# Hyena adapter kernel: loads moved across the two seams between its stages, stores awaited later

## The reference, cut to what matters

```python
def reference(x, ...):
    n = layernorm(x)
    proj = (n @ in_proj_w + in_proj_b).reshape(B, L, C, 3)
    v = depthwise_conv3(proj[..., 0], short_w) + short_b       # along the sequence
    coefs = MLP(pos)                                           # three layers, GELU; (L, C, 2)
    conv = irfft(rfft(v, 2L) * rfft(coefs[..., 1], 2L))[:L]    # the last of two orders decides
    x = x + (proj[..., 2] * conv) @ out_w + out_b
    Wsel, bsel = W[ids], b[ids]                                # 8 of 32 adapters
    return x + einsum('k,kod,bsd->bso', weights, Wsel, layernorm(x)) + weights @ bsel
```

## Time and profile before

| | |
|---|---|
| median of 3 runs | 2428.93 us (2424.77 to 2429.24) |
| profiled execution, its own time | 2427.41 us |
| its span | 2425.2 us |
| first stage and preparation | to 1013.7 us |
| middle, first to last matmul of its groups | 1027.1 to 1442.0 us |
| last stage, from its first matmul | 1455.0 us |
| granted TensorE clock, mean | 0.979 |

### The profile page before, as it was taken

One profiled execution on the slowest core, in us unless ns is written; L12 is line 12 of the kernel. 1 busy time (PEld: TensorE's weight loads), 2 busy tenths in 40 slices (PEclk: granted clock), 3 DMA queues, 4 the chain that ended last, 5 costly groups with the idle time before them and its releaser, 6 DMA issues. The chain is left out here.

```text
span 2425.2 us, 39710 instructions
## 1 busy us (share of the span) xinstructions
PE 2317.4 (96%) x12804; PEld 1602.1 (66%) x12804; DVE 1553.6 (64%) x2188; ACT 843.5 (35%) x1151; POOL 942.7 (39%) x1189
## 2 busy tenths in 40 slices
PE   6779999999999999779999988999999999999998
PEld 2257777777777777534444435777777777777776
DVE  5834444343434444257777767888888888888886
ACT  3334444444444444334444441222222222222222
POOL 1322222222222222100000006777777777777774
PEclk9879999999999999889999998999999999999999
DMA  5534545445444546489999988766666556665653
GB/s 184 217 100 139 186 165 178 160 154 196 156 160 145 190 153 212 158 337 356 361 355 358 359 315 257 227 182 177 179 177 181 174 175 179 175 176 177 179 179 103
DMA packets 180517, 496.60 MB, mean 205 GB/s; under 512 B 19419, under 2 KB 19740, under 8 KB 159332
## 3 DMA queue, kind: packets, MB, share of 16 engines
q1 hardware_dynamic: 150756, 395.10, 50.7%
q10 hardware_dynamic: 29696, 100.68, 11.5%
HBM read 276.27 MB, written 219.43 MB: 204 GB/s over the span
## 5 line engine op out<-in xcount | busy, mean ns | idle before, releaser
L1055 DVE TENSOR_TENSOR m_m<-m_psA,m_spec 128x1024 f32<-128x1024 f32 x256 | 295.4, 1216 | 132.0 <-PE m_psA L960 128.6
L709 POOL TENSOR_TENSOR vl<-v,vh 128x512 fp32r<-128x512 f32 x128 | 165.2, 1291 | 390.0 <-ACT vh L663 390.0
L1222 ACT ACTIVATE b_zh<-b_psT 128x512 fp32r<-128x512 f32 x128 | 76.5, 597 | 636.8 <-PE b_psT L1271 636.8
L977 PE MATMUL m_psW<-m_m,mats 64*64 64x512 f32 x2048 | 249.6, 593 | 0.0
L960 PE MATMUL m_psA<-m_xin,mats 64*64 64x512 f32 x1536 | 203.9, 602 | 30.5 <-DMA m_xin<-spec_f 13.5
L181 PE MATMUL psV<-wvh,nth 128*128 128x512 f32 x512 | 213.6, 417 | 0.6 <-DVE ntl L791 0.6
L810 DVE TENSOR_TENSOR gto<-psG,bgr 128x512 f32<-128x512 f32 x128 | 87.7, 685 | 195.5 <-PE psG L183 195.4
L181 PE MATMUL b_psO<-woh,b_oh 128*128 128x512 f32 x512 | 211.2, 412 | 0.0
L181 PE MATMUL b_psF<-wfh,b_zh 128*128 128x512 f32 x512 | 207.6, 406 | 2.8 <-DVE b_zl L1324 2.8
L1191 POOL TENSOR_TENSOR b_corr<-b_edge,b_v 128x512 f32<-128x512 f32 x128 | 199.2, 1556 | 14.5 <-DMA b_edge<-edge_f 14.4
L182 PE MATMUL b_psF<-wfl,b_zh 128*128 128x512 f32 x512 | 201.3, 393 | 0.0
(11 more groups left out here) (122 smaller groups left out, 4494.6 us busy)
## 6 DMA issues: line engine op xcount, KB each, us to landing
spec<-fs1o SPq DMA_DIRECT2D x64, 1024.0 KB, 8.8
spec<-m_wo ACTq DMA_DIRECT2D x64, 1024.0 KB, 8.4
b_fin<-spec SPq DMA_DIRECT2D x128, 512.0 KB, 4.6
m_xin<-spec SPq DMA_DIRECT2D x31, 2048.0 KB, 11.8
xg<-in_L_attn_x_dram SPq DMA_DIRECT2D x64, 512.0 KB, 6.1
gate_d<-gto SPq DMA_DIRECT2D x32, 1024.0 KB, 3.9
b_gin<-gate_d SPq DMA_DIRECT2D x128, 256.0 KB, 3.6
b_xin<-in_L_attn_x_dram SPq DMA_DIRECT2D x256, 128.0 KB, 3.2
```

Source lines behind the costliest of these rows:

```text
L709: pool.tensor_tensor(vl[:, t % 2], v[:, t % 2], vh[:, t % 2].bitcast(F32), ALU.subtract).then_inc(v_lo, 1)
L977: mm = pe.matmul(psW[pair % 2][half[slot], q, :], ws[slot][half[q]], m[half[q], pair % RM, part, slot, :], start=part == 0, stop=part == 1)
L1055: dve.tensor_tensor(m[:, (k - 2) % RM, part], psA[k % RA][:], spec[:, par, part], ALU.mult).then_inc(m_done, 1)
```

## The change

- xin, mats and the store tile of the middle ("wide") are allocated once, on the right side of SBUF, for front and middle; front's fs1o and the middle's m_wo are the same memory.
- load_first_groups, in front's list with lag 11, at tiles 2 and 5 of the last sequence: it loads mats and, for groups 0 and 1, spec_f and the seven batches that are stored by then. Batch 7 of both is loaded at the start of the middle, after a wait on the spec1 stores.
- front's SP no longer waits for the spec1 and gate stores at its end.
- The four pieces of group 0's load and load_consts are gone. out_w is loaded at step 0 of the last pass, behind group 30's load (load_w), and split during group 31: the high part by ACT (w_high), the low part by POOL.
- Behind group 31's load SP issues s4, the first row of v0, the edge rows of two tiles (EARLY), the two bias rows, the identity, and gate and x of two tiles; then, after waits, ad_mix and b_fin of two tiles. Their tiles are held from the middle to the last stage. The middle's own waits at its end are gone.
- ad_mix is turned in the last stage, in steps 1 and 3 of the first sequence (turn_w, w_high, w_low), in psF and in the memory of b_res. The other seven rows of v0 are loaded at tiles 9 to 15 of the first sequence.

```diff
--- before.py
+++ after.py
     def front(fc, mc):
...
-            s1o = sb("fs1o", [P, 2, 2, SUB, C])
+            s1o = mc["wide"].rearrange("p s (h t) c -> p s h t c", h=2)
...
+                def load_first_groups(b, t):
+
+                    if not (isinstance(b, int) and b == B - 1 and t in (2, 5)):
+                        return
+                    g = (2, 5).index(t)
+                    if g == 0:
+                        for slot in range(2):
+                            sp.wait_ge(s_stored[slot], 32 * (B - 1) * Q // 2)
+                        sp.dma_start(mc["mats"][:], consts["mid"]).then_inc(mc["mats_in"], 16)
+                    rows = slice(g * P, (g + 1) * P)
+                    sp.dma_start(mc["xin"][:, g, B], spec_f[rows]).then_inc(mc["early_in"][g], 16)
+                    sp.dma_start(mc["xin"][:, g, 0:B - 1], spec1[rows, 0:B - 1]).then_inc(mc["early_in"][g], 16)
...
-                pipelined(sp, B, T, [(load_x, 0), (save_v0, 5), (load_adapter, 6), (store_gate, 8), (store, 9), (store_mix, 11)])
+                pipelined(sp, B, T, [(load_x, 0), (save_v0, 5), (load_adapter, 6), (store_gate, 8), (store, 9), (store_mix, 11), (load_first_groups, 11)])
                 sp.wait_ge(ad_stored, 32)
-                for slot in range(2):
-                    sp.wait_ge(s_stored[slot], 32 * B * Q // 2)
-                    sp.wait_ge(g_stored[slot], 16 * B * Q // 2)
                 sp.wait_ge(v0_out, 16 * B)
...
     def middle(bc, mc):
...
             @block.sync
             def _(sp):
-                sp.dma_start(mats[:], consts["mid"]).then_inc(small_in, 16)
+                for slot in range(2):
+                    sp.wait_ge(mc["s_stored"][slot], 32 * B * Q // 2)
+                for g in range(2):
+                    sp.dma_start(xin[:, g, B - 1], rows_of(spec1, g)[:, B - 1]).then_inc(last_in[g], 16)
+                for slot in range(2):
+                    sp.wait_ge(mc["g_stored"][slot], 16 * B * Q // 2)
...
+                def load_w(i, s):
+
+                    if isinstance(i, int) and i > 0 and s == 0:
+                        sp.dma_start(wraw[:], out_w.rearrange("(k p) c -> p k c", p=P)).then_inc(w_in, 16)
+
+                pipelined(sp, GROUPS // 2, S, [(load, 0), (load_w, 0)])
+
+                sp.dma_start(bc["s4"][:], consts["s4"]).then_inc(bc["s4_in"], 16)
+                sp.dma_start(bc["v0_first"][:], first_v[0].rearrange("(a c) -> a c", a=1).partition_broadcast(P)).then_inc(bc["v0_in"], 16)
+                for t in range(EARLY):
+                    for q in range(2):
+                        sp.dma_start(bc["edge_a"][:, t, q], edge_f[q][:, t * C:(t + 1) * C]).then_inc(bc["edge_in"][t], 16)
+                sp.dma_start(bc["bor"][:], out_b.rearrange("(a c) -> a c", a=1).partition_broadcast(P)).then_inc(bc["rows_in"], 16)
+                sp.dma_start(bc["bfr"][:], ad_bias).then_inc(bc["rows_in"], 16)
+                sp.dma_start(bc["ident"][:], consts["ident"]).then_inc(bc["ident_in"], 16)
+                for t in range(EARLY):
+                    sp.dma_start(bc["gin"][:, t], gate_d[0, t // SUB].rearrange("p (s c) -> s p c", s=SUB)[t % SUB]).then_inc(bc["g_in"][t], 16)
+                    for h in range(2):
+                        sp.dma_start(bc["xin"][h * N1:(h + 1) * N1, t], by_tile(x[0])[h, :, t]).then_inc(bc["x_in"][t], 16)
+                sp.wait_ge(low, 1)
+                sp.dma_start(wraw[:], ad_mix).then_inc(bc["ad_in"], 16)
+                for par in range(2):
+                    sp.wait_ge(stored[0][par], 16 * GROUPS // 2)
+                for t in range(EARLY):
+                    sp.dma_start(bc["fin"][:, t], spec3.rearrange("(r h t) b c -> b t r h c", h=2, t=T)[0, t]).then_inc(bc["f_in"][t], 16)
+
+            @block.gpsimd
+            def _(pool):
+                pool.wait_ge(high, 1)
+                pool.tensor_tensor(bc["wol"][:], wraw[:], bc["woh"][:].bitcast(F32), ALU.subtract).then_inc(low, 1)
...
+                        if k == GS - 1 and at_first(i, s, 2):
+                            pe.wait_ge(last_in[par], 16)
...
-                pe.wait_ge(consts_in, 16 * CONSTS)
-                pe.wait_ge(m_done, 2 * GROUPS * PAIRS)
-                for d in range(CT):
-                    for ot in range(CT):
-                        mm = pe.transpose(psA[d // 2][:, d % 2, ot * P:(ot + 1) * P], ad_raw[:, ot, d * P:(d + 1) * P], bc["ident"][:])
-                    mm.then_inc(turned, 1)
...
+                def w_high(i, s):
+
+                    if isinstance(i, int) and i > 0 and s == GS:
+                        act.wait_ge(w_in, 16)
+                        act.activation(bc["woh"][:], wraw[:], ACT.Copy).then_inc(high, 1)
+
+                pipelined(act, GROUPS // 2, S, [(spectrum, 0), (out_early, 2), (out_last, 3), (w_high, 3)])
...
+            TURN_AT = (1, 3)
...
+                def load_v0(b, t):
+
+                    if isinstance(b, int) and b == 0 and t >= T - B + 1:
+                        k = t - (T - B)
+                        sp.dma_start(v0[:, k], first_v[k].rearrange("(a c) -> a c", a=1).partition_broadcast(P)).then_inc(v0_in, 16)
...
+                def turn_w(b, t):
+                    for d in turned_at(b, t):
+                        if d == 0:
+                            pe.wait_ge(bc["ad_in"], 16)
+                        if d >= 2:
+                            pe.wait_ge(wf_lo, d - 1)
+                        for ot in range(CT):
+                            mm = pe.transpose(psF[d % 2][:, ot * P:(ot + 1) * P], res[:, ot, d * P:(d + 1) * P], ident[:])
+                        mm.then_inc(wf_ps, 1)
...
+                    if isinstance(b, int) and b * T + t == 0:
+                        pe.wait_ge(wf_lo, CT)
...
-                pipelined(pe, B, T, [(conv_pair, 0), (adapt, 5), (turn_z, 4), (turn_o, 1), (project, 2)])
+                pipelined(pe, B, T, [(conv_pair, 0), (turn_w, 0), (adapt, 5), (turn_z, 4), (turn_o, 1), (project, 2)])
...
+                def w_low(b, t):
+                    for d in turned_at(b, t):
+                        dve.wait_ge(wf_hi, d + 1)
+                        dve.tensor_tensor(wfl[:, d], psF[d % 2][:], wfh[:, d].bitcast(F32), ALU.subtract).then_inc(wf_lo, 1)
...
-                pipelined(dve, B, T, [(gate, 1), (residual, 3), (z_low, 4), (o_low, 1), (finish, 5), (bias_x, 0)])
+                pipelined(dve, B, T, [(gate, 1), (residual, 3), (z_low, 4), (o_low, 1), (finish, 5), (bias_x, 0), (w_low, 0)])
```

More of the change, by code:

```diff
@@ L33 @@
 BR = 32
+D = 4
+EARLY = 2
 def stage_matrices():
@@ L498, in _, with front @@
                         w_lows(LOW_AT.index(t))
-    def front(fc):
+    def front(fc, mc):
         with ExitStack() as st:
@@ L826, in _, with middle @@
                 pipelined(dve, B, T, [(nt_low, 3), (v_bias, 4), (moments, 0), (g_bias, 4), (mix, 9)])
-    def middle(bc):
+    def middle(bc, mc):
         with ExitStack() as st:
@@ L899, in load @@
                         return
                     par = s // GS
-                    if at_first(i, s):
-                        for k, piece in enumerate(PIECES):
-                            src = rows_of(spec1, 0)[:, piece] if k else rows_of(spec_f, 0).rearrange("p (b c) -> p b c", b=1)
-                            sp.dma_start(xin[:, par, piece], src).then_inc(first_in[k], 16)
-                        return
-                    if not at_first(i, s, 2):
-                        sp.wait_ge(a_ps, (group(i, s) - 1) * PAIRS)
+                    sp.wait_ge(a_ps, (group(i, s) - 1) * PAIRS)
@@ L1020, in out_copy @@
                         act.wait_ge(w_out, n + 1)
-                        act.dma_start(rows_of(spec3, group(i, s))[:, batches], wo[:, par, batches]).then_inc(stored[par], 16)
+                        act.dma_start(rows_of(spec3, group(i, s))[:, batches], wo[:, par, batches]).then_inc(stored[pair // 2][par], 16)
                 def out_early(i, s):
@@ L1136, in no, with early, edge, turned_at @@
                 return b * T + t
+            def early(b, t):
+                return isinstance(b, int) and b == 0 and t < EARLY
+            def edge(q, t):
+                return edge_a[:, t, q] if t < EARLY else edge_b[:, t - EARLY, q]
+            TURN_AT = (1, 3)
+            def turned_at(b, t):
+                if isinstance(b, int) and b == 0 and t in TURN_AT:
+                    return range(2 * TURN_AT.index(t), 2 * TURN_AT.index(t) + 2)
+                return ()
             @block.sync
@@ L1151, in load_gate @@
                 def load_gate(b, t):
+                    if early(b, t):
+                        return
                     if old(b, t, 2):
@@ L1347, in hyena_adapter_kernel, with hold_right @@
         prep(fc)
-        front(fc)
+        both = ExitStack()
+        def hold_right(name, shape, dt=F32):
+            return both.enter_context(nc.sbuf_tensor(name, shape, dt, side="right"))
+        hold_right("right_pad", [P, 8])
+        mc = {
```

(20 more changed lines are left out.)

120 lines of the change are left out of this document (49 added, 71 removed).

## The result

| | before | after |
| --- | --- | --- |
| median of 5 runs, us | 2428.93 (2422.22 to 2429.48) | 2407.67 (2405.93 to 2411.45) |
| ratio, 95% interval | | 0.9928 (0.9916 to 0.994) |
| span of the profiled execution | 2425.2 | 2404.1 |

Of 2428.93 us the ratio is 17.5 us (14.6 to 20.4); 25.9 were forecast. The two medians lie 21.3 us apart. Faster, as forecast, and by less than forecast by either figure.

A forecast was written before the change was run, and what follows sets the result against it. PE, busy 96%, bounds the kernel, so only the two seams between stages can give time: 23.8+1.8=25.6 us off 2427.4 gives 2401.8, or 2403 us from the median; 2400 to 2406 (52%), 2395 to 2411 (more than 8 in 10).

The forecast's parts named there:

- second seam: From the middle into the last stage: 2.0 less, 1.4 back, 1.2 less, together 1.8 us less (2 more to 6 less).
- Stores awaited later: End of the first stage: SP skips its wait for spec1 and gate stores, PE starts 10.1 us earlier (9.1 to 11.1).
- Group 2: Start of the middle: the 11.05 us stall for its load goes, and 2.6 us of restart at half clock with it.
- out_w before group 31: End of the middle: out_w's 1 MB delays group 31's load by 5.1 us, stalling PE 3.0 us (0 to 6.9).
- The tail: End of the middle: 4.1 MB behind group 31's load are free; the first two conv tiles land at 1453 (1451 to 1455).
- The split on POOL: During group 31: POOL subtracts out_w's low part in 5.2 us; nothing charged for DVE working beside it.
- rival C: During group 31: POOL's 5.2 us shut DVE out, costing 1.9 us: 2405 us; chance 5%.
- The earlier rise of the clock: Start of the last stage: PE's clock may rise before the first projection, 0 to 2.3 us less, taken as 1.2.
- A: Second seam gives 4 to 7 us more, without group 31's stall or at full clock: 2396 to 2399; chance 20%.
- B: Before group 31: out_w costs its full 4.3 us and the clock falls: 2406 to 2409; chance 17%.
- D: First seam: group 2 or batch 7 still late as added loads push the last stores: 2408 to 2414; chance 4%.
- E: Slower: the middle becomes DMA-bound; 0.85 us more per group cancels the gain, 1.2 us gives 2439; chance 2%.

## Why the prediction was right and wrong

The forecast beside what the traces gave, the 1.55 us of the preparation taken out:

| stretch | gain forecast | gain measured |
| --- | --- | --- |
| first seam, PE's start | 10.1 | 10.1 |
| to the load of group 31 | 23.8 | 22.4 |
| from there to the second pair | 3.2 | 1.6 |
| second to third pair | -1.4 | -4.4 |
| second seam (the two rows above) | 1.8 | -2.9 |
| all | 25.6 | 19.6 |

*Stores awaited later*: right. PE's start moved by 11.66 us, 10.1 without the preparation; the wait put back costs 6.45 of them. Batch 7 was issued at 1021.35, landed 3.1 us later and was on time; moving groups 0 and 1 cost nothing in the first stage, whose length from psV to its last matmul is 871.9 and 871.8 us.

*Group 2*: right, no stall; its load landed in 10.6 us. The 2.6 us of the restart came back only as 0.6. The prediction subtracted the restart at half clock from the distance of groups 2 and 3 and did not ask what else would lie in the loop's first turn. Before, that turn ran when the DMA engines had little to do (111 GB/s from 1068 to 1078), since nothing was left to load after the stall; with the stall gone it falls beside full DMA engines (share 1.01, 426 GB/s) and PE waits. That the hole is the price of full DMA engines is shown (it is there in all versions with them, 1.5 to 2.1 us, the kernel before with late constants among them, and gone in the one profiled execution in which the stores are left out). That PE waits for its own instructions is the reading that fits: the releaser is "issue", and a packet of the instruction queue goes before it each time. In the change it starts at 1049.60 and PE resumes at 1052.10; in all ten executions with the hole PE resumes 2.2 to 2.5 us after such a packet starts, and so it does at the second wait of the change's repetition (1038.35 and 1040.59). There the packet starts 33.4 to 34.8 us after the middle's first matmul; with the stores left out it starts after 30.7 us, and PE comes to that place without a wait. No run moves the instructions themselves, so this stays a reading. The queue's 35 packets hold 0.57 MB, 16 KB each. By the Trainium skill, Advanced Engine Details and Errata, section "ISA Cache", a sequencer's cache line is 16 KB, 256 instructions; the packet size agrees.

*out_w before group 31*: mechanism right, size wrong. The stall was 0.77 us in one execution and 0.3 in the other, instead of 3.0, and leaving it away was worth 1.0 to 1.7. The 14.2 us that its load took are 1.7 more than before, not 5.1: group 31's load got more than the share by which the prediction reckoned. From its issue to its landing the SP queue had 62.0% of the engine time, not the 52.0% of the earlier trace rows, and the engines moved more in all than at this place before:

```profile
1412.80:1426.00 13.20, 13.20 (x128) 5.24 (x123) 10.10 (x10) 5.93 (x6) 0.00 (x0) 1.00 0.97 355
1388.50:1403.00 14.50, 13.90 (x128) 5.21 (x120) 11.41 (x11) 6.64 (x8) 0.00 (x0) 1.00 1.02 428
```

The first row is before, the second after: 355 and 428 GB/s. Why the share was larger was not tested.

*The tail*: here the prediction lost what it had won. It assumed 3.9 us for group 31's store and 40.5 us from group 31's load to the first conv tile (1453 less 1412.5). Measured were 8.4 and 42.0, though the stall in front was 2 us shorter. The 4.1 MB called free because nothing of the middle stood behind them on SP were not free: they share the DMA engines (385 GB/s and a share of 1.01 from 1398 to 1430) with the store that the conv tiles wait for. The queue order was read, the engines' load was not. Moving one megabyte out gave 1.0 us (out_w) and 1.8 to 2.0 us (b_s); issuing ad_mix behind the conv tiles gave 3.1. What followed the first conv tile was 1.0 us shorter than in the sum (10.9 us to turn_o(1), not 11.9), so that of the 2.0 us forecast up to turn_o(1) 1.5 came.

*The split on POOL*: right. POOL took 4.56 us for what was 5.2 in the sum, and DVE's product did not lengthen beside it (six in 6.88 us, mean 1.22 over the middle); rival C is out.

*The step that failed* is this one: "Two more w_low in step 3 stand in DVE's chain, which paces the third pair: 1.4 us back". Measured were 4.4 us back. The sum counted DVE's two subtractions, 1.29 us, and not what they wait for. Their operand is wfh. The product that w_high rounds to make it was there at 1449.7 by the timeline, but w_high stands behind norm on ACT, and norm waits for POOL until 1452.87; so w_high begins at 1453.59, DVE idles 2.03 us in front of w_low, the gate is late, PE idles 2.84 us on top of 0.88, and the clock falls at 1455. The projection of tile 2 then runs at half clock: 5.86 us from its transposes to the third pair, where the exchange of two names in ACT's order leaves 3.33. In all 4.4 us instead of 1.4, and the exchange gives them back (4.0 to 4.4 net). With it the second seam gains 1.5 us from group 31's load to the third pair (70.2 against 71.7 before), and the forecast of 1.8 would have stood.

Of the 6.0 us between 25.6 and 19.6 this step is 3.0. Up to group 31's load it is 1.4 (23.8 forecast, 22.4 measured): the loop's first turn lost 2.06, and the rest of that stretch gained 0.7 more than forecast. The earlier rise of the clock, taken at 1.2 us, gave 0.1: from turn_o(1) to the second pair PE took 5.38 us before and 5.29 after, most of it at half clock both times. The last 0.5 us is what the tail took.

The rivals: A and B looked for the error at group 31's stall, C at the shared port, D at group 2, E in the middle's rate. The stall was 0.3 to 0.8 us, near A's, and yet the second seam gave less than forecast and not more, so the small stall was luck that covered part of the loss; none of them named a chain inside the last stage. That the median came out at 2407.67, inside B's 2406 to 2409, is chance: B's full stall did not come. The range's upper end, 2411, hung on B and D and held the medians but not the ratio (0.9928 of 2428.93 is 2411.4).

## What to carry to other kernels

When operations are added to a step of a software pipeline, cost the chain of their operands on every engine's ordered list, not their own duration: an operand behind an operation that waits for a third engine costs more than the work. Loads that nothing waits for are free only if no store or load on the critical path is in flight on the same DMA engines at that time. When a stall is removed, look at what happened in its shadow (here, by the reading above, an instruction fetch) with idle resources, for it will now meet full ones.

## What the runs showed of the hardware

- The loop's first turn lost PE 1.5 to 2.1 us in ten executions (eight kernels) with full DMA engines, and 0.1 us (12.55 against 12.43) where they were idle. In the ten, PE resumed 2.2 to 2.5 us after a 16 KB packet of the instruction queue started.
- In the last stage of all twelve executions DVE's adds of two SBUF operands took 0.68 to 0.69 us when POOL was idle at their start, and up to 1.85 us when it was not. Its adds with a PSUM operand took 0.69 us at most beside the same POOL work, and the middle's product, which has one too, kept its length beside POOL's subtraction.
- A gap of 3.35 us at the first seam was enough for the granted clock to fall (0.76 in the microsecond in which PE started, 0.50 in the next), to the lower of the two levels, 1.2 GHz; it was back before group 1. In the last stage it fell (0.92 at 1455, 0.50 at 1456) when PE had 0.88 and 2.84 us of idle time with 0.66 us of transposes between, and did not fall where these were 0.86 and 0.35.
- With loads and stores mixed, one core's 16 DMA engines moved 428 GB/s over the 14.5 us from 1388.5, and 385 over the 32 us from 1398. The Trainium skill, Perfetto Trace Analysis, section "Roofline", gives about 435 GB/s as the bound of one core's 16 DMA engines; the trace agrees as far as it goes.
- The same preparation ended between 140.3 and 145.8 us in twelve executions, a spread larger than most effects above; with a marker behind it, two profiles of one kernel agreed within 0.4 us, and of another within 2.0 us.
